# Decoder layer on one Trainium2 core: attention products moved next to the scores in the tile loop, and a 128-column query projection

## The reference, cut to what matters

```python
x = layernorm(x + delta_net(x))                    # 8 heads of 128, a recurrence over 64 tokens
x = layernorm(x + cross_attention(x, ctx, seg))    # 16 heads, low-rank queries and keys, segment mask
x = layernorm(x + ffn(x))                          # 256 -> 1024 gate and up, silu, -> 256

# in cross_attention
q_c = q @ W_dq                                     # 256 -> 96, the query's down projection
scores = (q_nope @ k_nope + rope(q_c @ W_qr) @ k_rope) * scale
attn = softmax(where(good_keys, scores, NEG))
out = (attn @ v) @ W_o
```

## Time and profile before

| | us |
|---|---|
| median of three runs | 1147.1 |
| span of the profiled execution, first to last instruction | 1150.4 |
| TensorE busy in the span | 1101.5 (96%) |
| VectorE busy | 818.0 (71%) |
| ScalarE busy | 707.8 (62%) |
| one slot of the tile loop in the middle, four slots alike | 26.21 |
| TensorE busy in those 26.21 | 26.21 |
| VectorE / ScalarE busy in them | 15.87 / 11.73 |

### The profile page before, as it was taken

How to read it: one execution, slowest core, us unless ns; L and a number is a source line. 1 busy time by engine, 2 the same in 40 slices (tenths; PEclk the granted TensorE clock), 3 DMA queues, 4 the chain that set the end, 5 groups by cost and what they waited for, 6 DMA issues and landing times.

```text
span 1150.4 us, 28703 instructions
## 1 busy us (share of the span) xinstructions
PE 1101.5 (96%) x11420; PEld 763.6 (66%) x11420; DVE 818.0 (71%) x1429; ACT 707.8 (62%) x1243; POOL 472.0 (41%) x688
## 2 busy tenths in 40 slices
PE   8989799999999999999998899899999999999998
PEld 3444455555555555655554566679998999989987
DVE  5989769879779779779776756665666665655562
ACT  5777577687786777778676666554444444444433
POOL 1649484683882873964856512310000000110000
PEclk9999899999999999999998899999999999999999
DMA  4223345656565665666646332432222211112100
GB/s 131 56 63 88 86 73 86 132 106 101 126 94 110 124 115 96 133 138 143 141 88 219 103 121 66 134 95 51 51 53 67 51 48 47 47 48 50 29 19 10
DMA packets 164213, 101.82 MB, mean 89 GB/s; under 512 B 94289, under 2 KB 144593, under 8 KB 163185
## 3 DMA queue, kind: packets, MB, share of 16 engines
q1 hardware_dynamic: 162928, 99.78, 39.2%
q10 hardware_dynamic: 1152, 0.21, 0.1%
HBM read 62.72 MB, written 14.67 MB: 67 GB/s over the span
## 4 chain that ended last, share of the span: by engine, by line
PE 60%; DVE 12%; POOL 10%; issue 8%; ACT 4%; SPq 3%; DMA 3%; ACTq 0%; POOLq 0%; DVEq 0%
PE proj L581 13%; PE out L1792 5%; DVE conv L1213 5%; PE turned_v_chain L1792 5%; PE proj L1854 4%; PE turned_v_chain L1866 4%; PE proj L1731 4%; POOL inverse L1490 3%; POOL rank_one L1487 3%; PE gram L596 3%; PE gram L1766 2%; PE proj L1780 1%; PE turned_v_chain L587 1%; PE proj L1841 1%; PE out L605 1%
## 5 line engine op out<-in xcount | busy, mean ns | idle before, releaser
L1213 DVE SCALAR_TENSOR_TENSOR conv<-proj,kq_weights,conv 128x504 f32<-128x504 f32 (+2 forms) x261 | 189.7, 729 | 66.3 <-ACT conv L920 60.6
L581 PE MATMUL proj<-xT,vg_weights 128*128 128x512 f32 x384 | 194.1, 629 | 3.5 <-DMA vg_weights<-in_vg_w 2.2
L2109 POOL TENSOR_TENSOR rope<-rope_part,rope_part 128x512 f32<-128x512 f32 x32 | 42.1, 1336 | 321.5 <-DVE rope_part L2040 321.5
L581 PE MATMUL proj<-xT,kq_weights 128*128 128x512 f32 x348 | 167.7, 607 | 1.3 <-DVE conv L1213 1.0
L1213 DVE SCALAR_TENSOR_TENSOR conv<-proj,vg_weights,conv 128x504 f32<-128x504 f32 (+2 forms) x192 | 139.6, 728 | 26.4 <-ACT conv L920 23.3
L1490 POOL TENSOR_TENSOR inverse<-inverse,rank_one 128x30 f32<-128x30 f32 (+14 forms) x240 | 134.5, 560 | 18.8
L1487 POOL TENSOR_TENSOR rank_one<-inverse 128x30 f32<-128x30 f32 (+14 forms) x240 | 118.1, 492 | 22.9 <-DVE inverse L1274 8.0
L581 PEld LDWEIGHTS proj<-xT,kq_weights 128*128 128x128 f32 x348 | 62.4, 190 | 76.5 <-issue 64.0
L581 PEld LDWEIGHTS proj<-xT,vg_weights 128*128 128x128 f32 x384 | 66.9, 193 | 57.9 <-issue 50.0
L596 PEld LDWEIGHTS gram<-keys_q 128*64 128x64 f32 x896 | 56.8, 136 | 42.5 <-issue 24.9
L920 ACT ACTIVATE conv<-proj,kq_weights 128x512 f32<-128x512 f32 x87 | 59.6, 685 | 40.7 <-PE proj L581 40.3
(11 more groups left out here) (274 smaller groups left out, 2390.3 us busy)
## 6 DMA issues: line engine op xcount, KB each, us to landing
kq_weights<-in_kq_w SPq DMA_DIRECT2D x32, 390.0 KB, 6.5
vg_weights<-in_vg_w SPq DMA_DIRECT2D x32, 390.0 KB, 6.8
o_scratch<-oT SPq DMA_DIRECT2D x32, 256.0 KB, 2.2
o_in<-o_scratch SPq DMA_DIRECT2D x16, 512.0 KB, 4.1
o_rs<-o_rs_quarters SPq DMA_DIRECT2D x88, 64.0 KB, 6.1
diagonal<-gram_decayed SPq DMA_DIRECT2D x128, 32.0 KB, 2.0
inverse<-inverse SPq DMA_DIRECT2D x32, 128.0 KB, 2.8
q_first<-rope SPq DMA_DIRECT2D x128, 32.0 KB, 1.9
```

The costliest lines, as they stand in the source:

```text
L581: mm = e.matmul(bank(c, u)[:], w[:, (k * 3 + c % 3) * 128:(k * 3 + c % 3 + 1) * 128], xT[g][:, k, :], start=(k == 0), stop=(k == KD - 1))
L1213: e.scalar_tensor_tensor(acc(c, u)[:, :, back:], src[:, :, 0:S - back], weights(c, u)[:, j:j + 1], acc(c, u)[:, :, back:], ALU.mult, ALU.a ...
L2109: e.tensor_tensor(turned[half][:].rearrange("p b r q -> p r b q"), parts[2 * half][:], parts[2 * half + 1][:], op).then_inc(s_turned, 1)
```

## The change

In a slot of TensorE's list, `scores` of tile u2 moves from behind `out` to behind `down_q`, and the attention products of tile u3 move from behind `nope` to the place just ahead of these scores (a new function `mix`). The products go into banks b3 and b4, where their transposed softmax has stood, instead of b1 and b2. The waits follow: the products wait only for the two copies to `attT`, the scores wait for the mask of the tile before, the softmax transposes and nope for the copies to `ctxT`. ScalarE's list has the `attT` copies ahead of `silu(0)` and the `ctxT` copies ahead of `silu(1)` and the nope copies. VectorE's list has `hidden(0)` ahead of the mask. The down projection gets weights of 128 columns, the last 32 of them zeros.

```diff
-            ("w_out", [128, H, D]), ("w_dq", [128, KD, QC]), ...
+            ("w_out", [128, H, D]), ("w_dq", [128, KD, 128]), ...
...
-                        mm = e.matmul(out_bank(u)[0:QC, D:D + TILE], w_dq[:, k, :], x1T[:, k, :], start=(k == 0), stop=(k == KD - 1))
+                        mm = e.matmul(out_bank(u)[:, D:D + TILE], w_dq[:, k, :], x1T[:, k, :], start=(k == 0), stop=(k == KD - 1))
...
                 def nope(u):
                     if u >= AHEAD:
-                        e.wait_ge(s_attout, 2 * (u - 1))
+                        e.wait_ge(s_ctx, 2 * (u - 1))
...
-                    wait(e, s_ctx, 2 * (u - 1))
+                    wait(e, s_mask, 2 * u)
...
+                def mix(u):
+                    e.wait_ge(s_attout, 2 * (u + 1))
+                    for b in range(2):
+                        for h2 in range(2):
+                            mm = e.matmul((b3, b4)[b][64 * h2:64 * h2 + 64, :], kvtok[64 * b:64 * b + 64, u, :],
+                                          attT[64 * b:64 * b + 64, :, h2, :], start=True, stop=True)
+                    mm.then_inc(s_mix, 1)
...
-                        if live(u2):
-                            scores(u2)
...
                             e.wait_ge(s_soft, 5 * (u3 + 1))
                             wait(e, s_nopeout, 4 * (u3 + 2) if live(u3 + 1) else 0)
+                            wait(e, s_ctx, 2 * u3)
...
                         if live(u1) and u1 > AHEAD:
                             down_q(u1)
+                        if live(u3):
+                            mix(u3)
+                        if live(u2):
+                            scores(u2)
                         if live(u4):
                             ffn(1, u4)
...
-                        if live(u3):
-                            e.wait_ge(s_attout, 2 * (u3 + 1))
-                            wait(e, s_mask, 2 * (u3 + 2) if live(u3 + 1) else 0)
-                            for b in range(2):
...
                         if live(u2):
                             mask_scores(u2)
                             softmax_max(u2)
                         if live(u4):
-                            hidden(0, u4)
                             hidden(1, u4)
```

More of the change, by code:

```diff
@@ L215, in delta_phase @@
         tiles = {n: after_keys(f"t_{n}", shape) for n, shape in (
-            ("w_out", [128, H, D]), ("w_dq", [128, KD, QC]), ("w_qr", [QC, 4, 2, 128]), ("cos32", [128, S]), ("sin32", [128, S]),
+            ("w_out", [128, H, D]), ("w_dq", [128, KD, 128]), ("w_qr", [QC, 4, 2, 128]), ("cos32", [128, S]), ("sin32", [128, S]),
             ("w_qn", [QC, XH // 2, 2 * KVC]), ("kE", [128, TOK]), ("kO", [128, TOK]), ("keys", [128, S]))}
@@ L1921, in loop @@
                             copy_x1(u1)
[L1922 to L1925, removed]
                         if live(u3):
@@ L1934, in loop @@
                         if live(u4):
-                            silu(1, u4)
-                        if live(u1) and u3 != 0:
-                            copy_nope(u1)
+                            silu(0, u4)
+                        if live(u1) and u1 > AHEAD:
+                            copy_q(u1)
                         if live(u3):
@@ L1940, in loop @@
                             wait(e, s_cross, u3)
-                            for b, bk in enumerate((b1, b2)):
+                            for b, bk in enumerate((b3, b4)):
                                 e.activation(ctxT[:, :, b, :], bk.rearrange("p (h q) -> p h q", q=S), ACT.Copy).then_inc(s_ctx, 1)
-                        if u3 == 0:
+                        if live(u4):
+                            silu(1, u4)
+                        if live(u1):
                             copy_nope(u1)
@@ L2073, in loop @@
                             normalize(0, u1)
+                        if live(u4):
+                            hidden(0, u4)
                         if live(u2):
@@ L2194 @@
     arrays["w_kr"], arrays["w_krs"] = np.concatenate([kr, kr], axis=1), np.concatenate([krs, krs], axis=1)
-    arrays["w_dq"] = tile(i["xattn_W_dq"], QC)
+    arrays["w_dq"] = np.concatenate([tile(i["xattn_W_dq"], QC), np.zeros((128, KD, 128 - QC), np.float32)], axis=2)
     arrays["w_kvc2"] = np.concatenate([tile(i["xattn_W_kvc"], KVC)] * 2, axis=2)
```

## The result

| | before | after |
|---|---|---|
| median of four runs, us | 1147.4 | 1171.5 |
| ratio to before | | 1.021 (95% interval 1.018 to 1.023) |
| span of the profiled execution | 1150.4 | 1170.1 |
| one slot in the middle of the loop | 26.21 | 27.81 |
| TensorE's wait for x1, slots 4 to 15 | none | 18.3 in 12 waits |

The forecast was 1168 with a range of 1161 to 1177; the time rose by 24.1 us where 21.2 were worked out. The two profiles differ by 19.7 only, because the profile of before was itself a long execution: its span is 1150.4, and a second profile of the same kernel, taken later, spans 1146.7.

What follows compares the result with a forecast made beforehand. TensorE, busy throughout each 26.21 us slot, was taken as the bound. Twelve slots at 1.6 (19.2), head 1.2 and tail 0.8 sum to 21.2 us; on the median 1147.1 that gives 1168, range 1161 to 1177.

Steps and rivals of the forecast that it cites:

- The chain of x1: Slots 4 to 15: x1 ready 6.24 us after out's start, turn_x1 reached at 4.6; period 27.8 against 26.21, +1.6.
- The edges of the small groups: Products beside scores in TensorE's slot: four edges become three or two, 0.1 to 0.2 us saved; 0.1 taken.
- 128 columns: down_q at 128 instead of 96 columns: -0.05 to +0.05 us a slot, taken as 0.
- New waits: In the slots, for moved copies, mask, hidden(1) and rope transfers: zero to 0.7 us a slot, taken as 0.
- Head: Slots 2 and 3: x1 of tile 3 about 0.65 us sooner, rest of slot 3 2.0 longer less 0.1; +1.2.
- Tail: Slot 16: transfer wait of 1.58 us goes; waits for x2 1.0, attT 0.8, hidden(1) 0.7 come; +0.8.
- The rival with 8%: TensorE's clock falls to half at the new wait: 19 us more in all twelve slots, 10 in half; chance 8%.

Runs made afterwards that it cites:

- the scores alone: Kernel before with only the scores moved behind down_q, products left behind nope in b1 and b2: 1173.0 us, ratio 1.022.
- the scores back: Changed kernel with the scores put back behind out, ahead of turn_x1, products staying behind down_q: 1153.0 us, ratio 1.005.
- The swap: Changed kernel with the scores ahead of the products instead of behind them: 1168.4 us in one run.
- ffn(0) first: Changed kernel with ffn(0) ahead of turn_x1, down_q behind the scores and ScalarE's copies reordered: 1146.3 us, ratio 0.998.
- mask instructions earlier: Changed kernel with VectorE's four mask instructions moved from between the exponential and x1 to behind the rope parts: 1166.2 us, ratio 1.016.
- The two fastest versions: Changed kernel with ffn(0) ahead of turn_x1, 1146.3 us; the same with three orders changed behind the last out, 1144.7 us.

## Why the prediction was right, step by step

*The chain of x1.* Right in mechanism and size. Ready at 6.24 after out's start: 6.23. Period 27.8: 27.81. The wait is in all slots with an x1 and put down to VectorE's x. Shown by four versions: the scores alone bring it, the scores back take it away, a shorter queue shortens it by what the rows gave, and ffn(0) covers it.

*The edges of the small groups.* The sum took one edge of 0.1 off; the runs say two. With the scores alone moved a slot is 28.01, with the products beside them 27.81: 0.20. The swap shows that the step is free in both directions. The Trainium skill's rule in "TensorEngine Tiling (Array Packing)", Key Properties, that a change of tiling mode drains the engine, would leave three edges if 64x64 and 128x64 are two modes; the measurement shows two, and decides. Where no wait hides it, the gain is 0.15 (26.22 with the scores back, 26.07 with ffn(0) first), because the scores' old way out, into transposes, was the cheaper edge: 866.62 - 866.34 = 0.28 in the earlier trace rows, where the same two transposes behind out take 869.03 - 868.81 = 0.22.

In the period the forecast gave something back for these edges, and nothing was due. The period is the length of the loop, and TensorE's part of it, 12.59, had the products' two edges in it all along. The scores beside them add 2.01 and no edge, and turn_x1 behind its wait takes 0.28 instead of 0.22: 12.59 + 2.01 + 0.06 = 14.66, and with 13.15 it is 27.81, as measured. With the scores apart two edges more, 0.09 and 0.10, make 28.00; 28.01 was measured. The forecast's 27.8 differs only by roundings.

*128 columns.* Right at zero.

*New waits.* None in slots 4 to 15, as counted. ScalarE's attT copies of one slot, for the earlier trace rows:

```profile
844.53 1.08 ACT L1931 ACTIVATE attT<-gram 128x512 f32<-128x512 f32 x2
```

They end at 845.61, and the products start at 846.38 in that slot: 0.8 in hand, 0.6 in the forecast.

*Head.* x1 of tile 3 was forecast 0.65 sooner. From the second phase's first rope product to turn_x1 of tile 3 it took 762.60 - 740.11 = 22.49 before and 758.75 - 736.87 = 21.88 after: 0.61. What wasn't in the sum is the clock, below.

*Tail.* From the last turn_x1 to the end of the span it took 73.2 before and 76.0 after: 2.8. Of this the rest of slot 15, from turn_x1 to the down product, has 2.08 (16.05 before, 18.13 after), for the scores that now stand in it. Counted from turn_x1 to turn_x1 these are the 2.0 less 0.1 that the sum books in slot 3; again no edge was given back. Slot 16, from down product to down product, was 0.59 longer (20.18 and 20.77) where the sum had 0.8. The wait of 1.58 for the transfers is gone, as forecast; the wait for x2 is 0.85, those for attT and hidden(1) are 0.53 and 0.47 (1.0, 0.8 and 0.7 forecast):

```profile
1116.70 0.44 PE L1818 MATMUL turned_v_chain<-ident,x 128*128 128x128 f32 x2 [0.85 <-DVE x L2009]
...
1120.33 1.09 PE L1801 MATMUL gram<-attT,kvtok 64*64 64x512 f32 x8 [0.53 <-ACT attT L1931]
...
1127.67 1.16 PE L1792 MATMUL turned_v_chain<-x2T,t_w_gate 128*128 128x128 f32 x8 [0.47 <-DVE hid L2048]
```

*The clock.* The rival with 8% held in one place of thirteen. Behind the longest wait, in slot 3, the clock fell; in the twelve later slots it didn't.

```profile
758.75 0.44 PE L1740 MATMUL turned_v_chain<-ident,x 128*128 128x128 f32 x2 [2.02 <-DVE x L2009]
759.02 1.39 PE L1792 MATMUL out<-x2T,t_w_gate 128*128 128x128 f32 x8
760.20 1.91 PE L1792 MATMUL out<-x2T,t_w_up 128*128 128x128 f32 x8
```

```profile
760.00:764.00 4.00, 4.00 (x24) 2.96 (x24) 0.42 (x1) 2.52 (x5) 0.00 (x0) 0.62 0.00 0
```

The step from turn_x1 of tile 3 to that of tile 4 took 29.39 where the next ones take 27.81: 1.6 us of the missing ones. From the first rope product to the end the second phase took 433.2 after and 410.3 and 410.2 in the two profiles of before: 23 us, of which the sum had 21.2 and the clock 1.6. The last microsecond between 23 and the 24.1 of the runs isn't explained; the medians of before in three sessions lie 1.1 apart.

## What to carry to other kernels

On an engine that is busy all the time, a block of work that needs nothing may be the cover of a chain that runs on the other engines. Before it is moved, read off when the next waiting instruction's operand is ready, as an offset from the work that starts its chain, and compare it with the offset at which the instruction will come: here 6.24 against 4.6. If the chain closes into a loop, its length is the new period, and putting other free work of at least the gap's length in the same place (with the copies that this work needs moved up as well) gives the whole gap back.

## What the runs showed of the hardware

Neighbouring groups of 64-column products in 64x64 and 128x64 shape cost no more than the sum of their parts, in either order, while a step between them and products of 128 columns costs 0.09 to 0.10 us, and the step from the scores to transposes 0.06.

TensorE's clock fell to half at some waits and not at others. In the slots, 12 waits of 1.5 us in each of three versions (the changed kernel, scores only, swapped) and of 1.2 in one (mask instructions earlier) left it at 1.00. At the loop's head it fell at a wait of 2.02 (0.85 us after its end in the changed kernel, before its end with the scores alone moved), 0.9 and 1.2 us after the waits of 2.17 and 2.28 ahead of out (mask instructions earlier, and swapped), and after two waits of 1.23 and 1.20 close together (scores back); in that last version it fell again 0.7 us after the wait of 2.85 in slot 16. So each of the five waits of over 2 us that the profiles show in the second phase had a fall with it, and the waits of 1.58 and 1.59 had none. With the scores alone moved it also fell at 734.8, at the place where before's first profile shows its fall. The two fastest versions have no head wait over 1.24 and no fall. In the first profile of before it fell at 736.7 without the second one showing it, so a fall can also come or stay away in one and the same kernel: 1.6 us or more between executions that have the same waits there. What decides it the runs don't show.
